# Conditioned layer norms of a graph network: scale and shift as one float32r product over 128 rows

## The chip, the cores and the metric

One core of one Trainium2 chip. The metric is device microseconds of one execution of the whole program; the kernel before takes 2460.31 us (median of 3 runs, 2457.22 to 2461.17).

## The reference, cut to what matters

The program is a chain of four graph networks, each followed by an expert network, on 625 nodes of width 512 (five tiles of 125 nodes). The change concerns the third graph network: four blocks, each with two layer norms whose scale and shift come from a 16-wide condition per node.

```python
emb = jnp.concatenate([jnp.sin(ph), jnp.cos(ph)], axis=-1)
cond = jax.nn.silu(emb @ f_w1 + f_b1) @ f_w2 + f_b2            # (625, 16)
def _cond_layer_norm(x, cond, sw, sb, bw, bb):
    xn = (x - mu) * jax.lax.rsqrt(var + EPS)
    scale = cond @ sw + sb                                     # (625, 512)
    bias = cond @ bw + bb
    return xn * (1.0 + scale) + bias
for i in range(4):
    y = _cond_layer_norm(x, cond, s1_w[i], s1_b[i], b1_w[i], b1_b[i])
    y = _sparse_attention(y, src, dst, wq[i], bq[i], wk[i], bk[i], wv[i], bv[i], wo[i], bo[i])
    x = x + y
    y = _cond_layer_norm(x, cond, s2_w[i], s2_b[i], b2_w[i], b2_b[i])
    x = x + jax.nn.relu(y @ m_w1[i] + m_b1[i]) @ m_w2[i] + m_b2[i]
```

All of it is float32. 4 blocks, 2 norms and 5 tiles make 40 conditioned tiles, each with two products of a (125 x 17) by a (17 x 512) matrix.

## The kernel before, in words

Each network is a block of five hand-ordered instruction streams (TensorE = PE, VectorE = DVE, ScalarE = ACT, GpSimd = POOL, SyncE = SP, which issues the weight loads), joined by semaphores; a barrier ends a block. The order of each stream is the order of the Python code: nothing reorders it.

**The condition.** `b.GT` holds the condition turned, 16 rows and a row of ones, once on partitions 0 to 16 and again on 32 to 48 (ACT, L1472, late in the second layer of the graph network before). `b.affine[n]` holds, for norm n of a block, the weights and bias row of the scale on partitions 0 to 16 (columns 0 to 511) and those of the shift on 32 to 48 (columns 512 to 1023). SP loads them with two transfers (L1827, L1828, L1838, L1839; for the first block L1105), POOL sets the buffers to zero once (L1139), and ACT adds 1 to the scale's bias row in `plus_one` (L2053; L1511 for the first block).

**A conditioned tile** is one call of `cond(layer, n, t)` on PE (L1878; `next_condition(t)`, L1226, for the first three tiles): two float32 products with 32 rows each, one on row group 0 and one on row group 1 of the array (`tile_position=(32 * a, 0)`), into PSUM banks 6 and 7. DVE reads bank 6 in `norm_second` (L2173) and bank 7 in `norm_third` (L2179), which releases `y_ready`; the next `cond` waits for that, since the two banks are used again.

**The third graph network** (`l2_gnn_block`), per block of 4: values, keys and queries; a loop of i = 0 to 22 over 20 pairs (tile, head), in which PE does at step i `score(i)`, `turned(i - 2)` (five transposes), `attend(i - 3)`, at i = 7, 11, ... `project`, at i = 9, 13, 17, 21 `cond(layer, 1, 0..3)`. Beside it DVE adds the mask and takes the maximum (L2232), ACT does the exponential (L2083), DVE `normalise` (L2206), ACT copies the transposes (`turned_out`, L2090). At i = 9, 13, 17 ACT also takes the square root for the norm (`root`, L2060), which needs another function table, and then the exponential's again. After the loop come the dense layers with `cond(layer, 1, 4)` and `cond(layer + 1, 0, 0..4)` between their products. POOL adds bias rows to the residual in `add_row` (L1853).

**The end of the block before** (`l1_gnn_block`): six experts, each five products on PE (L1223) and five accumulations on DVE (`expert_added`, L1636); before the last expert's products PE does `next_condition(0)`; then `last_added`, `output_normed` and `next_norm` on DVE alternate with `next_turned` and `next_value` on PE for tiles 0 to 2.

Of the kernel before, what the change touches and what calls it, by code (L numbers as in the profile page):

```python
# [16 lines left out]
U32 = mybir.dt.uint32  # L17
ALU = mybir.AluOpType
# [80 lines left out]
class Program:  # L99
    def __init__(self, nc, ctx, args):  # L100
        self.nc, self.ctx, self.args = nc, ctx, args
        self.open = []

    def sb(self, name, shape, dt=F32):
        return self.ctx.enter_context(self.nc.sbuf_tensor(name, shape, dt))

# [868 lines left out]
FIRST_NORM = ("plus_one", "cond_mm", "y_ready", "var", "std", "xt_mm", "v_mm", "v_out", "c_act")  # L975
# [3 lines left out]
def l1_gnn_block(nc, p, b, A, hb):  # L979
# [8 lines left out]
                   "added", "cnt_max", "log_ready", "masked", "ovar", "ostd", "o_ready", "affine_zero", "pad_zero")  # L988
# [31 lines left out]
    emb_hidden = b.HT[0:16, 4, :]  # L1020
    c1, c2 = 6.28125, 0.0019340515136718750
# [23 lines left out]
    with nc.Block(no_gpsimd_drain=True) as block:  # L1045
        @block.sync
        def _(sp):
# [21 lines left out]
            sp.dma_start(b.emb_w[0:16, 16:80], A["L2_gnn_f_w2"]).then_inc(s["vec_in"], 16)  # L1069
# [49 lines left out]
        def _(pool):  # L1119
# [17 lines left out]
            pool.wait_ge(s["m2_mm"], T * NL)  # L1137
            for n in range(2):
                nc.gpsimd.memset(b.affine[n], 0.0).then_inc(s["affine_zero"], 1)  # L1139
# [3 lines left out]
        def _(pe):  # L1143
# [82 lines left out]
            def next_condition(t):  # L1226
                if t == 0:
                    pe.wait_ge(g2["plus_one"], 1)
                if t < 2:
                    pe.wait_ge(s["e_out"], E_OUT[NE - 2 + t, 1])  # L1230
                else:
                    pe.wait_ge(s["added"], T * (NE - 1) + 3)
                for i in range(2):
                    last = nc.tensor.matmul(b.ps[0:R, COND[t][i], :], b.GT[32 * i:32 * i + 32, t * R:(t + 1) * R],
                                            b.affine[0][32 * i:32 * i + 32, i * D:(i + 1) * D], start=True, stop=True,
                                            tile_position=(32 * i, 0))
                last.then_inc(g2["cond_mm"], 1)
# [24 lines left out]
            for layer in range(NL):  # L1262
# [51 lines left out]
                if layer == 1:  # L1314
                    pe.wait_ge(s["h1"], 1)
                    embed(b.emb_w[0:16, 16:80], emb_hidden, 64, "cond_mm")
# [50 lines left out]
        def _(act):  # L1367
# [72 lines left out]
            for layer in range(NL):  # L1440
# [29 lines left out]
                if layer == 1:  # L1470
                    act.wait_ge(s["cond_mm"], 1)
                    nc.scalar.activation(halves(b.GT[0:64, :]), b.slot(1)[0:64, :, 0:HF], ACT.Identity,  # L1472
                                         bias=b.cols[0:64, C["f_b2"]:C["f_b2"] + 1]).then_inc(s["cond"], 1)
# [35 lines left out]
            for n in range(2):  # L1509
                act.wait_ge(p.g2_affine[n], 32)  # L1510
                nc.scalar.activation(b.affine[n][0:32, 0:D], b.affine[n][0:32, 0:D], ACT.Identity,  # L1511
                                     bias=b.ident[0:32, 16:17]).then_inc(g2["plus_one"], 1)
# [12 lines left out]
        def _(dve):  # L1525
# [169 lines left out]
            for layer in range(NL):  # L1695
                for t in range(USED):
# [9 lines left out]
                    if layer == 1 and t % 6 == 5 and t < 60:  # L1706
                        angle_step(t // 6)
                for t in range(1, T, 2):
# [31 lines left out]
            for x in range(NE - 1):  # L1740
# [38 lines left out]
def l2_gnn_block(nc, p, b, A):  # L1779
# [5 lines left out]
                   "bo_added", "mb2_added", "stats")  # L1785
# [7 lines left out]
    OT = [b.W[:, 12288 + 512 * u:12288 + 512 * u + KD * R].rearrange("p (k n) -> p k n", k=KD) for u in range(2)]  # L1793
    GA, GB = (0, 3 * R), (3 * R, N)
# [22 lines left out]
    with nc.Block(no_gpsimd_drain=True) as block:  # L1817
        @block.sync
        def _(sp):
# [3 lines left out]
            clear_retired(sp, retired)  # L1823
            for layer in range(NL - 1):
# [13 lines left out]
                sp.dma_start(b.affine[1][0:17, 0:512], sb[:, 1024:1536]).then_inc(p.g2_affine[1], 16)  # L1838
                sp.dma_start(b.affine[1][32:49, 512:1024], sb[:, 1536:2048]).then_inc(p.g2_affine[1], 16)  # L1839
# [12 lines left out]
        def _(pool):  # L1852
# [9 lines left out]

            for layer in range(NL):
# [188 lines left out]
        def _(act):  # L2052
            def plus_one(layer, n):  # L2053
                act.wait_ge(p.g2_affine[n], 32 * (layer + 1))
                nc.scalar.activation(b.affine[n][0:32, 0:D], b.affine[n][0:32, 0:D], ACT.Identity,
# [1477 lines left out]
```

## Time and profile before

| what | value |
|---|---|
| median of 3 runs | 2460.31 us |
| span of the profiled execution, first to last instruction | 2460.5 us |
| PE busy | 2277.9 us (93%) |
| DVE, ACT, POOL busy | 1105.7, 700.9, 616.0 us |
| mean granted TensorE clock | 0.961 |
| third graph network, 1050 to 1735 us: PE busy | 677.9 of 685 us |
| PE instructions of `cond` (L1884) | 148, 41.6 us |

The span is counted from the program's first instruction; all times of rows below are on that axis. A float32 product appears as two pairs of LDWEIGHTS (PEld) and MATMUL (PE), so a conditioned tile is four MATMUL rows. A MATMUL's recorded duration includes the time until its last column has left the array; how fast PE gets through a row of products is read from the distances of their starts.

### The profile page before, as it was taken

The page shows a single profiled execution, that of the slowest core. Times are in us where ns is not written, and L with a number is a line of the kernel's source. Part 1 is how long each engine was busy: PE and PEld are TensorE (multiplying, and loading weights), DVE is VectorE, ACT ScalarE, POOL GpSimd, SP SyncE. Part 2 cuts the span into 40 slices and gives each one's busy share as a digit, 9 for nine tenths or more (in the row PEclk, how much of TensorE's full clock was granted, in tenths as well). Part 3 has the DMA queues.
Part 4 walks back from the last instruction along what each step waited for, and adds up shares of the span by engine and source line. Part 5 has one row for each costly group of instructions (what it writes and reads, how often), then busy time and mean ns, then how long its engine had stood idle before and what let it go on. Part 6 is the DMA issues. An engine that isn't in the chain of part 4 may idle for free. (4 is left out here: it accounts for less than half of the span.)

```text
span 2460.5 us, 35289 instructions
## 1 busy us (share of the span) xinstructions
PE 2277.9 (93%) x12133; PEld 1471.8 (60%) x12133; DVE 1105.7 (45%) x2643; ACT 700.9 (28%) x1366; POOL 616.0 (25%) x625
## 2 busy tenths in 40 slices
PE   5798969999999999999999999999997896989998
PEld 4475547766766765566566576576653333567775
DVE  8733885545545546735325325335442223530102
ACT  0422333323333323225225135135201111112111
POOL 0463666506515520010100100101123442111110
PEclk9898989999999998999999999999989997979999
DMA  3122027517516533010110110110037646458885
GB/s 91 49 68 78 1 64 222 151 31 225 152 43 212 152 100 113 1 61 38 51 68 1 58 60 1 57 52 1 21 141 246 230 169 208 108 217 320 306 298 181
DMA packets 70260, 285.73 MB, mean 116 GB/s; under 512 B 19274, under 2 KB 19402, under 8 KB 62158
## 3 DMA queue, kind: packets, MB, share of 16 engines
q1 hardware_dynamic: 35771, 189.60, 22.0%
q0 software_dynamic: 32448, 91.31, 12.3%
q10 hardware_dynamic: 1872, 2.56, 0.4%
q8 instruction: 107, 1.75, 0.3%
q14 instruction: 62, 0.51, 0.1%
HBM read 407.54 MB, written 26.23 MB: 176 GB/s over the span
## 5 line engine op out<-in xcount | busy, mean ns | idle before, releaser
L86 PE MATMUL ps<-XT,W 128*128 128x250 f32 (+1 forms) x1200 | 335.4, 435 | 3.5 <-ACT XT L1420 1.6
L86 PEld LDWEIGHTS ps<-XT,W 128*128 128x128 f32 x1200 | 229.0, 193 | 106.4 <-issue 22.3
L1150 PE MATMUL ps<-XN,W 128*128 128x512 f32 x498 | 256.8, 598 | 2.6 <-ACT GT L1472 2.6
L1856 POOL TENSOR_TENSOR H<-H,RB 125x512 f32<-125x512 f32 x40 | 50.5, 1266 | 723.9 <-DVE XN L2179 611.6
L86 PE MATMUL ps<-W,HT 128*128 128x512 f32 (+1 forms) x312 | 141.5, 608 | 0.8 <-ACT HT L3293 0.5
L86 PEld LDWEIGHTS ps<-HT,W 128*128 128x128 f32 x1088 | 126.3, 195 | 8.8 <-issue 7.7
L86 PE MATMUL ps<-HT,W 128*128 128x128 f32 x1088 | 126.6, 278 | 0.8 <-DVE HT L3304 0.8
L2567 POOL DMA_INDIRECT result_rows<-KT,LOGC x61 | 61.9, 1016 | 257.0 <-DVE KT L3324 211.7
L1126 POOL DMA_INDIRECT XT<-node_rows,LOGC x81 | 77.3, 954 | 173.8 <-DMA node_rows<-V 122.2
L1288 PEld LDWEIGHTS ps<-P,QT 128*128 128x128 f32 x672 | 89.2, 194 | 44.5 <-issue 44.5
L1288 PEld LDWEIGHTS ps<-P,KT 128*128 128x128 f32 x672 | 88.1, 192 | 39.7 <-issue 39.7
L3293 ACT ACTIVATE HT<-ps,lcols 128x128 f32<-128x128 f32 x136 | 50.1, 368 | 211.1 <-PE ps L86 211.1
L1288 PEld LDWEIGHTS ps<-P,XT 128*128 128x128 f32 x648 | 85.2, 193 | 41.7 <-issue 41.6
L2720 PE MATMUL ps<-W,HT 128*32 128x320 f32 x824 | 109.0, 445 | 0.0
L2232 DVE CUSTOM_DVE_ANT_0 P<-ps,LOGC 125x626 f32<-125x626 f32 x80 | 64.6, 807 | 96.0 <-PE ps L94 96.0
L86 PE MATMUL ps<-HT,V 125*128 125x125 f32 x800 | 102.7, 275 | 0.0
L86 PEld LDWEIGHTS ps<-W,HT 128*128 128x128 f32 (+1 forms) x312 | 58.8, 193 | 72.7 <-issue 67.8
L94 PE MATMUL ps<-KT,QT 128*125 128x313 f32 x320 | 98.8, 430 | 0.0
L1126 POOL DMA_INDIRECT QT<-node_rows,LOGC x84 | 79.7, 949 | 65.5 <-PE ps L1288 41.6
L86 PEld LDWEIGHTS ps<-HT,V 125*128 125x128 f32 x800 | 95.7, 192 | 0.3
L2083 ACT ACTIVATE P<-P,nmax 125x626 f32<-125x626 f32 x80 | 65.4, 818 | 98.9 <-DVE nmax L2237 98.8
L1126 POOL DMA_INDIRECT KT<-node_rows,LOGC x84 | 79.4, 945 | 56.0 <-PE ps L1288 45.1
(654 smaller groups left out, 4422.7 us busy)
## 6 DMA issues: line engine op xcount, KB each, us to landing
W<-in_L_ffn_Wgud SPq DMA_DIRECT2D x103, 896.0 KB
W<-in_L_ffn_w SPq DMA_DIRECT2D x36, 2048.0 KB, 7.9
W<-in_L_gnn_Wqkv SPq DMA_DIRECT2D x4, 3072.0 KB, 10.0
W<-in_L_gnn_W SPq DMA_DIRECT2D x5, 2048.0 KB, 14.4
H<-in_L_ffn_Wgud SPq DMA_DIRECT2D x11, 896.0 KB
XN<-in_L_ffn_Wgud SPq DMA_DIRECT2D x11, 896.0 KB
V<-in_L_ffn_Wgud SPq DMA_DIRECT2D x11, 896.0 KB
P<-in_L_ffn_Wgud SPq DMA_DIRECT2D x11, 896.0 KB
```

Of the source, the lines that this page charges most:

```text
L86: last = nc.tensor.matmul(out, lhs(k), rhs(k), start=(k == 0), stop=(k == nk - 1))
L94: last = nc.tensor.matmul(slot[0:m, a, 0:HF], lhs(k), rhs(k)[:, a * HF:(a + 1) * HF], start=(k == 0), stop=(k == nk - 1))
L1126: nc.gpsimd.indirect_dma_start(edges[n % GR], None, hb, bass.IndirectOffsetOnAxis(ap=b.slot_src[:, t:t + 1], axis=0)).then_inc(arrived[n % ...
L1150: nc.tensor.matmul(b.ps[:, n % PR, :], b.EAT[:, t * 128:(t + 1) * 128], We[layer], start=True, stop=True)\
L1288: last = nc.tensor.matmul(sums[:, k * 128:][:, bass.ds(off, R)], edges[n % GR][:, k * 128:(k + 1) * 128], hot[n % HR], start=False, stop=F ...
L1856: ins = nc.gpsimd.tensor_tensor(b.H[0:R, t, :], b.H[0:R, t, :], b.RB[0:R, at:at + D], ALU.add)
L2083: nc.scalar.activation(P[j % 5], P[j % 5], ACT.Exp, bias=b.nmax[0:R, j:j + 1], accum_out=b.den[0:R, j:j + 1]).then_inc(s["exp"], 1)
L2232: v.tensor_tensor_reduce(out=halves(P[i % 5]), in0=b.slot(0)[0:R, :, 0:HF], in1=halves(b.LOGC[0:R, t, :]), scale=1.0, scalar=-3e38, op0=AL ...
L2567: self.nc.gpsimd.indirect_dma_start(self.rows, bass.IndirectOffsetOnAxis(ap=self.b.slot_row[:, sl:sl + 1], axis=0), out, None, bounds_chec ...
L2720: last = nc.tensor.matmul(b.ps[QUARTER[j], 1 + u % 2, 0:2 * HE], xT[u % 2][:, k, QUARTER[j]], Wgu[4 * (u % WR) + j][:, k, :], start=(k == ...
L3293: nc.scalar.activation(hT[u][:, m, :], b.ps[:, 1 + m % 4, 0:128], ACT.Relu, bias=r.bias[u][:, m:m + 1]).then_inc(s["hidden_ready"], 1)
```

## The change

The condition and the affine weights are kept in two parts each: a high part, rounded to float32r, and the rest, which float32r holds exactly. The four row groups of 32 partitions hold, for the condition, high, rest, high, rest, and for the weights high, high, rest, rest, so that one product over 128 rows sums all four partial products. Scale and shift are then two products, one behind the other, on the whole array. The 1 of `1 + scale` becomes a row of the weights. `plus_one` goes.

Instead of it, per norm: SP loads 18 rows by 1024 columns into each of four row groups of a staging buffer (four transfers in place of two); DVE rounds all 128 x 1024 into `b.affine[n]` (`affine_high`); POOL subtracts on the lower 64 partitions (`split_affine`), after which `cond` may start. The condition is split once, on DVE, in the third layer of the network before. The last network's product with `b.GT` uses its 8 rows alone.

```diff
+    def rounded(self, name, like, shape, column=0):
+        return self.nc.alloc_sbuf_tensor_at(name, shape, F32R, offset=self.start_of[like] + 4 * column)
...
+            sp.wait_ge(s["staged_zero"], 1)
             for n in range(2):
-                sp.wait_ge(s["affine_zero"], n + 1)
-                for part in range(2):
-                    at = 1024 * n + 512 * part
-                    sp.dma_start(b.affine[n][32 * part:32 * part + 17, 512 * part:512 * part + 512],
-                                 A["L2_gnn_sb"][0, :, at:at + 512]).then_inc(p.g2_affine[n], 16)
+                for i in range(4):
+                    sp.dma_start(staged[n][32 * i:32 * i + 18, :], A["L2_gnn_sb"][0, :, 1024 * n:1024 * (n + 1)])\
+                        .then_inc(p.g2_affine[n], 16)
...
+            nc.gpsimd.memset(kt[:, 0:2048], 0.0).then_inc(s["staged_zero"], 1)
             for n in range(2):
-                nc.gpsimd.memset(b.affine[n], 0.0).then_inc(s["affine_zero"], 1)
+                pool.wait_ge(s["affine_high"], n + 1)
+                nc.gpsimd.tensor_tensor(b.affine[n][64:128, :], staged[n][64:128, :], b.affine[n][64:128, :],
+                                        ALU.subtract).then_inc(g2["affine_split"], 1)
...
             def next_condition(t):
                 if t == 0:
-                    pe.wait_ge(g2["plus_one"], 1)
+                    pe.wait_ge(s["cond_split"], 2)
+                    pe.wait_ge(g2["affine_split"], 1)
...
+                    if layer == 2 and t == 5:
+                        v.tensor_copy(b.cond_pair[:, :], cond_rows).then_inc(s["cond_high"], 1)
+                    if layer == 2 and t in (11, 17):
+                        dve.wait_ge(s["cond_high"], 1)
+                        lo = 32 if t == 11 else 96
+                        v.tensor_tensor(b.cond_pair[lo:lo + 32, :], cond_rows[lo:lo + 32],
+                                        b.cond_pair[lo:lo + 32, :], ALU.subtract)\
+                            .then_inc(s["cond_split"], 1)
...
+                if x == 4:
+                    for n in range(2):
+                        dve.wait_ge(p.g2_affine[n], 64)
+                        v.tensor_copy(b.affine[n], staged[n]).then_inc(s["affine_high"], 1)
             last_added(0)
...
                 sp.wait_ge(s["cond_mm"], norm(layer, 0, T - 1))
-                sp.dma_start(b.affine[0][0:17, 0:512], sb[:, 0:512]).then_inc(p.g2_affine[0], 16)
-                sp.dma_start(b.affine[0][32:49, 512:1024], sb[:, 512:1024]).then_inc(p.g2_affine[0], 16)
+                sp.wait_ge(s["affine_split"], 2 * layer + 2)
+                for i in range(4):
+                    sp.dma_start(staged[32 * i:32 * i + 18, :], sb[:, 0:1024]).then_inc(p.g2_affine[0], 16)
...
+            def split_affine(layer, n):
+                pool.wait_ge(s["affine_high"], 2 * layer + n - 1)
+                pool.wait_ge(s["bo_added"], T * layer + 3 if n else T * layer)
+                nc.gpsimd.tensor_tensor(b.affine[n][64:128, :], staged[64:128, :], b.affine[n][64:128, :],
+                                        ALU.subtract).then_inc(s["affine_split"], 1)
...
                     for t in range(T):
                         add_row(layer, n, t)
+                        if t == 2 and n == 0 and layer:
+                            split_affine(layer, 1)
+                    if n == 0 and layer < NL - 1:
+                        split_affine(layer + 1, 0)
...
             def cond(layer, n, t):
                 if t == 0:
-                    pe.wait_ge(s["plus_one"], 2 * layer + n + 1)
+                    pe.wait_ge(s["affine_split"], 2 * layer + n + 1)
...
-                    last = nc.tensor.matmul(b.ps[0:R, 6 + a, :], b.GT[32 * a:32 * a + 32, t * R:(t + 1) * R],
-                                            b.affine[n][32 * a:32 * a + 32, a * D:(a + 1) * D], start=True, stop=True,
-                                            tile_position=(32 * a, 0))
+                    last = nc.tensor.matmul(b.ps[0:R, 6 + a, :], b.cond_pair[:, t * R:(t + 1) * R],
+                                            b.affine[n][:, a * D:(a + 1) * D], start=True, stop=True)
...
+            def affine_high(layer, n):
+                dve.wait_ge(p.g2_affine[n], 64 * (layer + 1))
+                v.tensor_copy(b.affine[n], staged).then_inc(s["affine_high"], 1)
...
                     if i:
                         normalise(layer, i - 1)
+                    if layer and i == 2:
+                        affine_high(layer, 1)
+                    if not final and i == 6:
+                        affine_high(layer + 1, 0)
```

Three places in the order of the streams. **DVE, end of the block before**: L1636 are the experts' accumulations, L1758 an independent mask step; the last of the six L1636 in a row is the first tile of the last expert. Before:

```order
1160 L1758 SCALAR_TENSOR_TENSOR LOGC<-P,LOGC 125x3130
1161 L1636 SCALAR_TENSOR_TENSOR X<-ps,gates,X 125x512 x6
1162 L1648 BN_STATS stats<-X 125x6
1163 L1649 BN_AGGR mv<-stats 125x2
1164 L1636 SCALAR_TENSOR_TENSOR X<-ps,gates,X 125x512
```

Now (L1647 is the line that was L1636):

```order
1163 L1778 SCALAR_TENSOR_TENSOR LOGC<-P,LOGC 125x3130
1164 L1647 SCALAR_TENSOR_TENSOR X<-ps,gates,X 125x512 x5
1165 L1783 CAST affine_pair<-KT 128x1024 x2
1166 L1647 SCALAR_TENSOR_TENSOR X<-ps,gates,X 125x512
1167 L1659 BN_STATS stats<-X 125x6
```

The two roundings stand behind all five accumulations of the fifth expert and ahead of the first of the sixth. **PE at the same place**, L1238 (was L1223) the experts' products, L1250 `next_condition`, L1257 transposes, L87 (was L86) values; the order of the rows is that of before:

```order
3262 L1238 MATMUL ps<-W,HT 125x512 x5
3263 L1250 MATMUL ps<-affine_pair,cond_pair 125x512 x2
3264 L1238 MATMUL ps<-W,HT 125x512 x5
3265 L1250 MATMUL ps<-affine_pair,cond_pair 125x512 x2
3266 L1257 MATMUL ps<-ident,XN 128x125 x4
3267 L1250 MATMUL ps<-affine_pair,cond_pair 125x512 x2
3268 L87 MATMUL ps<-W,XT 125x512 x4
```

What moved is what row 3263 waits for: the subtraction on POOL instead of an addition on ACT. **POOL** from the end of that block into the first two blocks of the third network; L1884 is `add_row`, L1152 and L1894 are the subtractions:

```order
119 L1148 MEMSET KT 128x2048
120 L1152 TENSOR_TENSOR affine_pair<-KT,affine_pair 64x1024 x2
121 L1155 MEMSET KT 128x4
122 L1056 UNCONDITIONAL_BRANCH
123 L1879 UNCONDITIONAL_BRANCH
124 L1898 MEMSET W 128x1024
125 L1884 TENSOR_TENSOR H<-H,RB 125x512 x5
126 L1894 TENSOR_TENSOR affine_pair<-W,affine_pair 64x1024
127 L1884 TENSOR_TENSOR H<-H,RB 125x512 x8
128 L1894 TENSOR_TENSOR affine_pair<-W,affine_pair 64x1024
```

Before, POOL had two memsets of 128 x 1024 in place of the first two rows and nothing between the additions of L1856.

## Rows read from the trace of the kernel before

**Rows 1.** Windows: length, busy us of PE, PEld, DVE, ACT, POOL, clock, DMA.

```profile
1015.00:1050.00 35.00, 32.21 (x85) 14.48 (x84) 27.21 (x46) 6.46 (x14) 0.00 (x0) 0.90 0.00 0
1050.00:1225.00 175.00, 171.77 (x769) 110.58 (x767) 75.21 (x184) 63.02 (x129) 17.59 (x14) 1.00 0.12 43
```

**Rows 2.** Waits of PE, 1040 to 1730: us in total, times, longest.

```profile
PE ps L1939 <- ACT HT L2090: 4.2, 12, 0.3
```

**Rows 3.** Timeline of PE in the first block: start us, us, line, xcount.

```profile
1178.31 5.21 PE L86 MATMUL ps<-XT,W 128*128 128x375 f32 x16
1183.36 1.02 PE L86 MATMUL ps<-W 128*125 128x512 f32 x2
...
1187.93 5.31 PE L86 MATMUL ps<-XT,W 128*128 128x375 f32 x16
1193.17 1.12 PE L1884 MATMUL ps<-W,GT 32*125 32x512 f32 x4
1194.23 1.98 PE L1973 MATMUL ps<-W,HT 128*125 128x512 f32 x4
```

**Rows 4.** 512 columns: line L307 (ns min/median/max, first to last start); timeline, float32.

```profile
L307 PE MATMUL ps<-H x8: 374/374/425, 59.6 to 61.2; 1*125 1x512 bf16 x8
...
1023.56 4.45 PE L1223 MATMUL ps<-W,HT 128*125 128x512 f32 x10
```

**Rows 5.** Timeline, all engines, around step 9 of the loop, first block.

```profile
1126.34 0.82 ACT L2083 ACTIVATE P<-P,nmax 125x626 f32<-125x626 f32 x1 [1.28 <-DVE nmax L2237]
1126.86 1.12 PE L1884 MATMUL ps<-W,GT 32*125 32x512 f32 x4
1127.27 1.28 ACT L2060 ACT_TABLE_LOAD   x1
1128.76 0.67 ACT L2090 ACTIVATE HT<-ps 125x625 f32<-125x625 f32 x1
1129.58 0.78 PE L1939 MATMUL ps<-ident,P 125*125 125x125 f32 x5 [0.34 <-ACT HT L2090]
```

**Rows 6.** Timeline of the end of the block before.

```profile
1024.62 4.18 DVE L1636 SCALAR_TENSOR_TENSOR X<-ps,gates,X 125x512 f32<-125x512 f32 x5 [0.99 <-PE ps L1223]
1027.94 1.12 PE L1234 MATMUL ps<-W,GT 32*125 32x512 f32 x4
1029.00 4.56 PE L1223 MATMUL ps<-W,HT 128*125 128x512 f32 x10
1036.71 1.09 PE L1242 MATMUL ps<-ident,XN 125*128 125x125 f32 x4 [2.11 <-DVE XN L1661]
1037.74 2.07 PE L1234 MATMUL ps<-W,GT 32*125 32x512 f32 x4
1039.74 5.52 PE L86 MATMUL ps<-W,XT 128*125 128x512 f32 x8
```

**Rows 7.** Groups by line and shape: busy us, mean ns.

```profile
L555 DVE COPY P<-CNT 125x626 f32<-125x626 f32 x5 | 2.4, 479 | 0.0
L2179 DVE SCALAR_TENSOR_TENSOR XN<-XN,rstd,ps 125x512 f32<-125x512 f32 x37 | 27.7, 748 | 1.3
L1856 POOL TENSOR_TENSOR H<-H,RB 125x512 f32<-125x512 f32 x40 | 50.5, 1266 | 723.9 <-DVE XN L2179 611.6 <-POOLq L1045 112.3
```

**Rows 8.** Timeline, POOL and DVE in the last block; all of L2206 (ns min/median/max).

```profile
1665.30 1.27 POOL L1860 TENSOR_TENSOR H<-H,X 125x512 f32<-125x512 f32 x1
...
1665.65 1.25 DVE L2206 TENSOR_SCALAR P<-P,den,row_has 125x626 f32<-125x626 f32 x1
...
L2206 DVE TENSOR_SCALAR P<-P,den,row_has x80: 604/606/1255, 1099.8 to 1700.4; 125x626 f32<-125x626 f32 x80
```

**Rows 9.** Timeline of DVE: step 7, step 3 (block 2), edge loop.

```profile
1116.11 0.81 DVE L2232 CUSTOM_DVE_ANT_0 P<-ps,LOGC 125x626 f32<-125x626 f32 x1 [1.23 <-PE ps L94]
...
1283.35 0.60 DVE L2206 TENSOR_SCALAR P<-P,den,row_has 125x626 f32<-125x626 f32 x1
...
787.32 0.69 DVE L1704 TENSOR_TENSOR KT<-KT,ps 128x512 f32<-128x512 f32 x1 [0.87 <-PE ps L1150]
```

More of the change, by code:

```diff
@@ L17 @@
 U32 = mybir.dt.uint32
+F32R = mybir.dt.float32r
 ALU = mybir.AluOpType
@@ L972, in l0_ffn_block @@
     close_retired(retired)
-FIRST_NORM = ("plus_one", "cond_mm", "y_ready", "var", "std", "xt_mm", "v_mm", "v_out", "c_act")
+FIRST_NORM = ("affine_split", "cond_mm", "y_ready", "var", "std", "xt_mm", "v_mm", "v_out", "c_act")
 FIRST_TILES = 3
@@ L1020, in l1_gnn_block @@
     emb_hidden = b.HT[0:16, 4, :]
+    kt = b.KT[:, :, :].rearrange("p k n -> p (k n)")
+    staged = [kt[:, 1024 * n:1024 * (n + 1)] for n in range(2)]
+    cond_rows = b.HT[:, 5, :]
     c1, c2 = 6.28125, 0.0019340515136718750
@@ L1233, in next_condition @@
                 for i in range(2):
-                    last = nc.tensor.matmul(b.ps[0:R, COND[t][i], :], b.GT[32 * i:32 * i + 32, t * R:(t + 1) * R],
-                                            b.affine[0][32 * i:32 * i + 32, i * D:(i + 1) * D], start=True, stop=True,
-                                            tile_position=(32 * i, 0))
+                    last = nc.tensor.matmul(b.ps[0:R, COND[t][i], :], b.cond_pair[:, t * R:(t + 1) * R],
+                                            b.affine[0][:, i * D:(i + 1) * D], start=True, stop=True)
                 last.then_inc(g2["cond_mm"], 1)
@@ L1471, in _ @@
                     act.wait_ge(s["cond_mm"], 1)
-                    nc.scalar.activation(halves(b.GT[0:64, :]), b.slot(1)[0:64, :, 0:HF], ACT.Identity,
-                                         bias=b.cols[0:64, C["f_b2"]:C["f_b2"] + 1]).then_inc(s["cond"], 1)
+                    nc.scalar.activation(halves(cond_rows), b.slot(1)[:, :, 0:HF], ACT.Identity,
+                                         bias=b.cols[:, C["f_b2"]:C["f_b2"] + 1]).then_inc(s["cond"], 1)
             turned_out(2)
@@ L1508, in _ @@
                     nc.scalar.activation(b.LOGC[0:R, :, :], b.P[0:R, :, :], ACT.Ln).then_inc(s["log_ready"], 1)
[L1509 to L1512, printed above, removed]
             row_root("ovar", "ostd", b.std, b.mv, 0)
@@ L1707, in _ @@
                         angle_step(t // 6)
+                    if layer == 2 and t == 5:
+                        dve.wait_ge(s["cond"], 1)
+                        v.tensor_copy(b.cond_pair[:, :], cond_rows).then_inc(s["cond_high"], 1)
[5 more added lines that the diff above has]
+                            .then_inc(s["cond_split"], 1)
                 for t in range(1, T, 2):
@@ L1823, in _ @@
             clear_retired(sp, retired)
+            sp.wait_ge(s["staged_zero"], 1)
             for layer in range(NL - 1):
@@ L1861, in add_row @@
                 ins.then_inc(done, 1)
+            def split_affine(layer, n):
[3 more added lines that the diff above has]
+                                        ALU.subtract).then_inc(s["affine_split"], 1)
+                pool.wait_ge(s["affine_split"], 2 * layer + n + 1)
+            nc.gpsimd.memset(staged, 0.0).then_inc(s["staged_zero"], 1)
             for layer in range(NL):
@@ L2052, in _ @@
         def _(act):
-            def plus_one(layer, n):
-                act.wait_ge(p.g2_affine[n], 32 * (layer + 1))
-                nc.scalar.activation(b.affine[n][0:32, 0:D], b.affine[n][0:32, 0:D], ACT.Identity,
-                                     bias=b.ident[0:32, 16:17]).then_inc(s["plus_one"], 1)
             def root(layer, n, t):
@@ L2107, in _ @@
                         root(0, 0, 4)
-                if layer:
-                    plus_one(layer, 1)
                 for t in range(2):
@@ L2131, in _ @@
                     hidden_out(layer, m, M1A + m, GA, 0)
-                if not final:
-                    plus_one(layer + 1, 0)
                 root(layer, 1, 4)
@@ L3046, in _ @@
             for t in range(T):
-                nc.tensor.matmul(b.ps[0:R, B2_BANKS[t], :], b.GT[:, t * R:(t + 1) * R], B2, start=True, stop=True)\
+                nc.tensor.matmul(b.ps[0:R, B2_BANKS[t], :], b.GT[0:NE, t * R:(t + 1) * R], B2[0:NE, :], start=True,
+                                 stop=True)\
                     .then_inc(s["b2_mm"], 1)
@@ L3409, in build @@
         b.PT = ht[:, 0:T * NP].rearrange("p (t n) -> p t n", t=T)
-        b.affine = [b.W[:, 14336 + 1024 * n:14336 + 1024 * (n + 1)] for n in range(2)]
+        affine_pair = p.rounded("affine_pair", "W", [128, 2048], 14336)
+        b.affine = [affine_pair[:, 1024 * n:1024 * (n + 1)] for n in range(2)]
+        b.cond_pair = p.rounded("cond_pair", "GT", [128, NP])
         at = [0]
@@ L3457, in pad, with padded, affine @@
         return out
-    def twice(x, next_row):
-        out = np.zeros(64, f)
-        for at in (0, 32):
-            out[at:at + 16], out[at + 16] = x, next_row
-        return out
+    def padded(x, ones):
+        out = np.zeros(32, f)
+        out[:16], out[16:18] = x, ones
+        return out
+    def affine(i):
+        parts = []
+        for n, one in (("s1", 1), ("b1", 0), ("s2", 1), ("b2", 0)):
+            parts.append(np.concatenate([a[f"L2_gnn_{n}_w"][i], a[f"L2_gnn_{n}_b"][i][None], np.full((1, D), one, f)]))
+        return np.concatenate(parts, axis=1)
     freq = pad(np.tile(np.arange(1, 33, dtype=f) * f(TWO_PI / 16), 2))
@@ L3467, in _layout @@
             col(a["L0_gnn_be2"]), a["L0_ffn_b1"].T, freq, pad(a["L2_gnn_f_b1"]),
-            pad(twice(a["L2_gnn_f_b2"], f(1)))]
+            np.tile(padded(a["L2_gnn_f_b2"], f(1)), 4)[:, None]]
     out = {
@@ L3487, in _layout @@
         "L1_ffn_w2": np.concatenate(list(a["L1_ffn_w2"]), axis=1),
-        "L2_gnn_f_w1": a["L2_gnn_f_w1"], "L2_gnn_f_w2": np.stack([twice(x, f(0)) for x in a["L2_gnn_f_w2"]]),
-        "L2_gnn_sb": np.concatenate([np.concatenate([a[f"L2_gnn_{n}_w"], a[f"L2_gnn_{n}_b"][:, None, :]], axis=1)
-                                     for n in ("s1", "b1", "s2", "b2")], axis=2),
+        "L2_gnn_f_w1": a["L2_gnn_f_w1"], "L2_gnn_f_w2": np.stack([np.tile(padded(x, f(0)), 4) for x in a["L2_gnn_f_w2"]]),
+        "L2_gnn_sb": np.stack([affine(i) for i in range(4)]),
         "L2_gnn_Wqkv": np.stack([np.concatenate([rows(a[f"L2_gnn_w{n}"][i]) for n in "qkv"], axis=1)
```

20 lines of the change are left out of this document (13 added, 7 removed).

## Prediction, made before the run

> **What bounds the kernel now.** I read the page's busy shares first, then windows over the third graph network. The first of its four blocks shows PE busy 171.8 of 175 us at a granted clock of 1.00, the 2.4 GHz level, with DVE at 75 and ACT at 63 us [rows 1]. The list of who waits for whom confirms it: over the whole network PE loses 4.2 us in 12 waits of 0.3 us, all at the transposes L1939 on ACT's copies, and next to nothing else [rows 2]. So here a microsecond of PE time is a microsecond of the kernel, unless the PE time lies in front of one of those 12 waits. The last 35 us of the block before are different: clock 0.90 and DVE busy 27.2 us, a chain that passes between DVE and PE [rows 1].
>
> **What a conditioned tile costs.** Its four MATMUL rows start at 1193.17 and the next work at 1194.23: 1.06 us [rows 3]. Around it there is more. Sixteen float32 rows of 375 columns between ordinary neighbours go from 1178.31 to 1183.36, 5.05 us; sixteen such rows between two conditioned tiles take 1187.93 to 1193.17, 5.24 us. The 0.19 us are a pause ahead of the 32-row products and one behind them. **A tile costs 1.25 us.** Ten float32 rows of 512 columns take 4.45 us, 0.43 to 0.44 each [rows 4], so four in a row would be 1.7: the two products do run at the same time on their two row groups.
>
> **What it costs afterwards.** No float32r product is in this trace. The nearest below is bfloat16 with 512 columns: eight start between 59.6 and 61.2 us, 0.23 us each, in one row per product [rows 4]. The nearest above is float32, two rows of 0.43 or 0.86 us per product. Two products on the whole array, one behind the other, cost 0.46 us by the first and 1.72 by the second. I take 0.46, since splitting both factors in parts that the type holds exactly only makes sense if the array multiplies what it is given in one pass, and a product over all 128 rows has ordinary neighbours, so the pauses go. Were they to stay, 0.65. Gain per tile: 1.25 - 0.46 = 0.79 us, at least 0.60 if the pauses stay.
>
> The Trainium skill, TensorEngine Tiling (Array Packing), "Key Properties", says that a change of tiling mode drains the engine; the pauses of 0.19 us agree with it, and by it they go.
>
> **How many tiles pay.** 40 tiles, in three groups.
> - 12 pay nothing: those at i = 9, 13 and 17 in four blocks. At i = 9 ACT begins an exponential at 1126.34, before PE begins the tile (1126.86); ACT then loads a table (1127.27), takes the root, copies the transposes (1128.76), and only then may PE transpose again, at 1129.58 after 0.34 us of waiting [rows 5]. Nothing of that ACT chain waits for the tile. A shorter tile makes the wait 0.34 + 0.79 = 1.1 us and the transposes come at the same time. These are the 12 waits of [rows 2].
> - 25 pay in full: two at the start of the first block, four at i = 21, four `cond(layer, 1, 4)`, and fifteen of the next block's first norm. PE meets no wait behind them, and where it meets DVE's result (second tile of a norm) that result is counted from a product that moves forward with it. 25 x 0.79 = **-19.8 us**.
> - 3 lie at the end of the block before, and there something is added.
>
> **The end of the block before.** DVE ends the fifth expert at 1024.62 + 4.18 = 1028.80, while PE began the first conditioned tile already at 1027.94 [rows 6]: its weights had long been ready. Now they are ready only after DVE rounds (behind 1028.80) and POOL subtracts. Rounding 1024 columns: the copy L555 takes 0.48 us for 626 columns [rows 7], so 0.78; the upper bound is L2179's rate, 0.75 us per 512, so 1.5. Subtracting 1024 columns on POOL: twice 1.27 [rows 7], 2.5 us. The first tile starts at 1028.80 + 0.78 + 2.53 and 0.1 to hand over (0.15 between ACT's end and PE in [rows 5]), 1032.2, or at 1033.0 if POOL gets at the data only behind the second rounding; with 0.46 us for the tile the sixth expert's products start at 1032.7 to 1033.4 in place of 1029.00: 3.7 to 4.4 us late. All that follows hangs on them through DVE. Behind it one tile takes 2.07 us, twice the usual, and the next products 5.52 us for eight rows: the low clock level after PE's wait of 2.11 us [rows 6]. That tile shrinks by 1.1 to 1.5 us. The new PE wait of 4 us may call up the low level too, earlier; then the products behind are hit instead, which is worth 2 us either way. Net 0 to 5, I take **+2.5 us**.
>
> The Trainium skill, SBUF — State Buffer, "Who interferes with whom", says that VectorE and GpSimd share one port pair that an instruction holds as a whole. The trace agrees: L2206, 0.606 us in the median, took 1.25 us when POOL's L1860 had begun 0.35 us ahead of it [rows 8]. By this rule the later of the two starts, 1033.0, holds.
>
> **The rest, by what covers it.** Six roundings in the attention loops, at i = 2 and i = 6: DVE has waited 1.23 us for PE before the next step [rows 9], more than 0.78; at 1.5 us a step is 0.3 late, 1.8 us in all at most. Six subtractions on POOL, which is idle for 724 us around its 40 additions [rows 7]; the additions behind them are not wanted before the loop's end. SP gives out four transfers for two and now waits for the subtraction; behind that wait stand the next block's weights, wanted a block (175 us) later. ACT loses eight `plus_one`, for which PE does not wait today: nothing gained. Three DVE instructions in the edge loop of the block before, 0.5 to 0.9 us each by the rows of [rows 7], against a DVE wait of 0.87 us per edge [rows 9]: at most 0.3 us. The five last products with 8 rows have as many columns as before: nothing, or a pause or two. Together **+0.3 us** (0 to 2.5).
>
> **Sum.** 2460.5 - 19.8 + 2.5 + 0.3 = **2443.5 us**, 0.7% faster. The profiled span of 2460.5 us stands at the median of the runs (2460.31), so nothing is to be converted. 0.2% are 4.9 us, about what a measurement of this kernel tells from no change.
>
> **Rivals.**
> - *The float32r product costs what float32 costs.* Then the overlap of the two row groups is given up for nothing: 1.72 us per tile, 0.47 more on 25 tiles (11.8 us); on 12 the wait of 0.34 swallows all but 0.13 (1.6 us); the end of the block before gives 3.8. 2460.5 + 17.2 = **2477.7**, slower. It decides above 0.57 us per product, where 25 x (1.25 - 2p) equals the 2.8 us added. For it: no such row here; against it: the single pass that the split suggests. 0.08. The Trainium skill, TensorE: Matmul & The Clock Gate, "Part 3", counts matmuls on different row groups as simultaneous; the 1.06 us against 1.7 above agree, and it is what the change gives up.
> - *The change does half of what it says*: two rows, 0.43 us per product. 0.86 per tile, gain 0.39 x 25 = 9.8: **2453.5**. 0.08.
> - *POOL holds up the softmax.* The subtraction after i = 2 lasts till about 1284.0 by the same working, and L2206 starts at 1283.35 [rows 9]: it would be held 0.6 us, and PE wants the result a step later, about a microsecond on. If all six subtractions came through in full, 15 us: **2458**, no change. 0.05.
> - *The 12 tiles pay too*, because the ACT chain moves forward in some way that I do not see: 37 x 0.79 = 29.2: **2434**. 0.05.
>
> **Chances.** My forecast 0.74, its own range 2440 to 2451 (0.60 to 0.79 per tile, 0 to 5 and 0 to 2.5 us). Range to hold 8 in 10: 2438 to 2456, which takes in the half case and leaves out 0.18. Faster: 0.74 and 0.05 and half of the half case, 0.83. Same: the rest of that and POOL, 0.08. Slower: 0.09.
>
> **What would show it.** Right: 74 and 6 MATMUL rows for `cond` and `next_condition` in place of 148 and 12, with starts 0.21 to 0.23 us apart; sixteen rows of 375 columns between two tiles in 5.05 us; 12 waits on L2090's successor of about 1.1 us, 13 us in all; PE waiting some 4 us before the first tile at the end of the block before. Wrong: starts 0.43 or 0.86 us apart, the 12 waits still 0.3 us, or new waits of PE for the softmax at i = 4 or i = 8.

## The result, and the profile after

The changed kernel takes 2439.64 us (median of 4 runs, 2437.80 to 2444.14), the kernel before on the same chip 2459.65 us: a ratio of 0.9918, 95% interval 0.9906 to 0.9930, so 17 to 23 us or 0.7 to 0.9% faster. The forecast was 2443.5 us. The profiled execution is the fastest of the four: 2437.8 us, span 2436.1 us, against a span of 2460.5 before. That is a difference of 24.4 us, more than the medians show; where the surplus lies is settled below.

Lines have moved: `cond` is L1924 (was L1884), `next_condition` L1250 (L1234), the transposes of the softmax L1978 (L1939), ACT's copies of them L2124 (L2090), the division of the softmax L2236 (L2206).

**Conditioned tiles.** The groups by line of the changed kernel: engine, operation, count, then min/median/max duration in ns.

```profile
L1924 PE MATMUL ps<-affine_pair,cond_pair x74: 387/439/797, 1055.1 to 1700.1; 128*125 128x512 f32 x74
...
L1250 PE MATMUL ps<-affine_pair,cond_pair x6: 395/434/824, 1030.4 to 1040.2; 128*125 128x512 f32 x6
```

74 and 6 rows in place of 148 and 12: one row per product, so float32r is one pass. The recorded durations (387 to 824 ns) say nothing about their price; the distances do. PE in the first block, at the place of [rows 3]: start us, us, line, xcount.

```profile
1183.34 1.02 PE L1924 MATMUL ps<-affine_pair,cond_pair 128*125 128x512 f32 x2
1184.20 5.20 PE L87 MATMUL ps<-XT,W 128*128 128x375 f32 x16
1188.95 0.92 PE L1924 MATMUL ps<-affine_pair,cond_pair 128*125 128x512 f32 x2
1189.70 0.59 PE L2012 MATMUL ps<-W,HT 128*125 128x512 f32 x1
```

From the sixteen rows of 375 columns to the first product behind the tile it is 1189.70 - 1184.20 = 5.50 us. The same stretch in [rows 3] is 1194.23 - 1187.93 = 6.30. Less the 5.05 of the sixteen rows, a tile costs **0.45 us where it cost 1.25**. (Here the recorded starts mislead: the product at 1188.95 is stamped 0.03 us behind the last row of 375 columns, which itself needs 0.31.)

**The third network**, from its first conditioned tile to the first of its last five accumulations on DVE (1055.99 to 1728.69 before), in windows; columns as in [rows 1]. Before, then after:

```profile
1055.99:1728.69 672.70, 667.39 (x2969) 432.57 (x2970) 274.23 (x669) 243.00 (x490) 56.87 (x45) 1.00 0.11 41
```

```profile
1055.07:1709.04 653.97, 639.41 (x2895) 435.51 (x2896) 277.69 (x675) 239.17 (x484) 72.29 (x52) 1.00 0.12 44
```

18.7 us shorter at the same granted clock of 1.00, with 74 PE rows fewer. PE's busy time falls by 28.0 us, 9 more than the stretch does: those went into waits. PE's waits, 1040 to 1730 us, against [rows 2]:

```profile
PE ps L1978 <- ACT HT L2124: 13.6, 12, 1.1
...
PE ps L1924 <- PEq L1056: 1.1, 1, 1.1
```

The 12 waits behind the tiles of steps 9, 13 and 17 are 1.1 us now, 13.6 in all, and no wait for the softmax has appeared. The place of [rows 5], with ACT's table load:

```profile
1124.36 0.70 PE L1924 MATMUL ps<-affine_pair,cond_pair 128*125 128x512 f32 x2
1124.90 1.22 PE L95 MATMUL ps<-KT,QT 128*125 128x313 f32 x4
1124.94 1.28 ACT L2094 ACT_TABLE_LOAD   x1
...
1126.44 0.67 ACT L2124 ACTIVATE HT<-ps 125x625 f32<-125x625 f32 x1
1127.26 0.78 PE L1978 MATMUL ps<-ident,P 125*125 125x125 f32 x5 [1.14 <-ACT HT L2124]
```

**The end of the block before**, all engines, against [rows 6]:

```profile
1021.64 4.45 PE L1238 MATMUL ps<-W,HT 128*125 128x512 f32 x10
1022.70 4.18 DVE L1647 SCALAR_TENSOR_TENSOR X<-ps,gates,X 125x512 f32<-125x512 f32 x5 [0.99 <-PE ps L1238]
1026.80 1.28 DVE L1783 CAST affine_pair<-KT 128x1024 fp32r<-128x1024 f32 x2
1027.63 5.08 POOL L1152 TENSOR_TENSOR affine_pair<-KT,affine_pair 64x1024 fp32r<-64x1024 f32 x2 [85.92 <-DVE affine_pair L1783]
1030.38 0.70 PE L1250 MATMUL ps<-affine_pair,cond_pair 128*125 128x512 f32 x2 [4.29 <-issue]
1030.91 6.15 PE L1238 MATMUL ps<-W,HT 128*125 128x512 f32 x10
1039.24 0.65 PE L1257 MATMUL ps<-ident,XN 125*128 125x125 f32 x4 [1.68 <-DVE XN L1672]
1039.90 0.73 PE L1250 MATMUL ps<-affine_pair,cond_pair 128*125 128x512 f32 x2
1040.66 3.67 PE L87 MATMUL ps<-W,XT 128*125 128x512 f32 x8
```

PE stands still for 4.29 us until the first subtraction on POOL is done. The ten products behind the stop then run in part at the low clock (6.15 us in place of 4.56), while the tile and the eight products that had run in part at it before (2.07 and 5.52 us) take 0.73 and 3.67. In windows of ten microseconds the granted clock is 0.83 from 1030 on (part of it at 1.2 GHz, the lower of two levels) and 1.00, 2.4 GHz, from 1040 on:

```profile
1030.00:1040.00 10.00, 7.93 (x19) 3.63 (x19) 7.07 (x15) 0.96 (x4) 2.73 (x3) 0.83 0.00 0
1040.00:1050.00 10.00, 8.86 (x26) 3.99 (x26) 9.54 (x21) 2.39 (x6) 0.00 (x0) 1.00 0.00 0
```

From the fifth expert's first product to the third network's first tile it is 33.43 us here, 32.43 before: +1.0.

**What covers the rest.** The roundings and subtractions at the end of the block before and in the loops, and all divisions of the softmax: ns min/median/max, first to last start.

```profile
L1783 DVE CAST affine_pair<-KT x2: 682/683/684, 1026.8 to 1027.4; 128x1024 fp32r<-128x1024 f32 x2
...
L1152 POOL TENSOR_TENSOR affine_pair<-KT,affine_pair x2: 2352/2502/2651, 1027.6 to 1030.4; 64x1024 fp32r<-64x1024 f32 x2
...
L2241 DVE CAST affine_pair<-W x6: 684/686/686, 1112.5 to 1617.0; 128x1024 fp32r<-128x1024 f32 x6
...
L1894 POOL TENSOR_TENSOR affine_pair<-W,affine_pair x6: 2353/2358/2359, 1113.2 to 1617.7; 64x1024 fp32r<-64x1024 f32 x6
...
L2236 DVE TENSOR_SCALAR P<-P,den,row_has x80: 604/606/1044, 1097.5 to 1682.0; 125x626 f32<-125x626 f32 x80
```

### The profile page after: what moved, and what is told of

It is laid out like the page before. It is cut to its first block and busy times, and to the rows that moved or that the text cites. A ratio compares the mean times of both kernels' runs of the same rounds, so it can differ in the third digit from the quotient of the medians.

```text
span 2436.1 us, 35178 instructions
## 1 busy us (share of the span) xinstructions
PE 2245.6 (92%) x12053; PEld 1473.5 (60%) x12053; DVE 1111.6 (46%) x2654; ACT 695.9 (29%) x1358; POOL 637.6 (26%) x633
## 5 line engine op out<-in xcount | busy, mean ns | idle before, releaser
L87 PE MATMUL ps<-XT,W 128*128 128x250 f32 (+1 forms) x1200 | 333.7, 434 | 3.5 <-ACT XT L1435 1.6
L87 PEld LDWEIGHTS ps<-XT,W 128*128 128x128 f32 x1200 | 229.4, 193 | 100.1 <-issue 15.6
L87 PE MATMUL ps<-W,HT 128*128 128x512 f32 (+1 forms) x312 | 141.3, 607 | 0.8 <-ACT HT L3332 0.5
L1884 POOL TENSOR_TENSOR H<-H,RB 125x512 f32<-125x512 f32 x40 | 50.9, 1278 | 314.4 <-DVE XN L2209 314.1
L87 PEld LDWEIGHTS ps<-HT,W 128*128 128x128 f32 x1088 | 126.5, 195 | 8.8 <-issue 7.7
L87 PE MATMUL ps<-HT,W 128*128 128x128 f32 x1088 | 126.8, 278 | 0.8 <-DVE HT L3343 0.8
L87 PE MATMUL ps<-HT,V 125*128 125x125 f32 x800 | 102.7, 275 | 0.0
L87 PEld LDWEIGHTS ps<-W,HT 128*128 128x128 f32 (+1 forms) x312 | 58.6, 193 | 72.7 <-issue 67.7
L87 PEld LDWEIGHTS ps<-HT,V 125*128 125x128 f32 x800 | 95.7, 192 | 0.3
```

The lines of the kernel that those rows point to most:

```text
L87: last = nc.tensor.matmul(out, lhs(k), rhs(k), start=(k == 0), stop=(k == nk - 1))
L1884: ins = nc.gpsimd.tensor_tensor(b.H[0:R, t, :], b.H[0:R, t, :], b.RB[0:R, at:at + D], ALU.add)
```

## Experiments

**1. The changed kernel once more**: is the surplus of the first pair of profiles part of the change? No edit.

> The changed kernel once more. In the first pair of profiles the changed kernel is 24.4 us shorter. Theory: what the change itself does is 17 to 19 us (in the third network 18.7, at the end of the block before +1.0); the other 6.7 us lie in stretches in which the work is unchanged (1.9 ahead of the last experts, 4.8 behind the third network) and are differences between executions. Then this run's third network again takes 654 us from its first conditioned tile to its end, within 0.5, its span comes out anywhere from 2436 to 2444, and at least one of the other stretches differs from the first profile by a microsecond or more. Rival: the 6.7 us belong to the change (fewer loads, or another alignment of the later work). Then all stretches repeat within 0.5 us and the span is 2436 again.

Measured: 2442.81 us (median, 2436.09 to 2448.43), ratio to the kernel before 0.9921, interval 0.9906 to 0.9936; the profiled execution has a span of 2446.7 us. The third network takes 653.9 us again, within 0.1 of the first. All else moved: the fifth expert begins at 1024.54 (1021.64 in the first), the end of the block before takes 35.87 us (33.43), and from the end of the third network's last accumulation to the end of the program it is 709.1 us (703.7), with not a line of difference. So the surplus is not the change's. In the ten profiles of this study that last stretch, in which their code is the same but for line numbers (and, between the kernel before and all others, five products with 8 rows in place of 128), takes 701.9 to 710.7 us: a single profile can be several microseconds off in the whole, while the third network of the changed kernel repeats within a tenth of one.

At the end of the block before the low clock came the second time on the eight products of the values as well, which the first execution had run at the full clock:

```profile
1033.28 1.19 PE L1250 MATMUL ps<-affine_pair,cond_pair 128*125 128x512 f32 x2 [4.29 <-issue]
1034.27 6.23 PE L1238 MATMUL ps<-W,HT 128*125 128x512 f32 x10
...
1042.88 0.65 PE L1257 MATMUL ps<-ident,XN 125*128 125x125 f32 x4 [1.92 <-DVE XN L1672]
1043.54 0.73 PE L1250 MATMUL ps<-affine_pair,cond_pair 128*125 128x512 f32 x2
1044.30 5.37 PE L87 MATMUL ps<-W,XT 128*125 128x512 f32 x8
```

That is 1.7 us of the 2.4 that lie between the two executions; the granted clock of the same two windows is 0.66 and 0.83 here:

```profile
1030.00:1040.00 10.00, 6.72 (x13) 3.26 (x13) 4.58 (x10) 0.59 (x2) 5.11 (x3) 0.66 0.00 0
1040.00:1050.00 10.00, 8.04 (x22) 3.49 (x20) 9.47 (x21) 1.48 (x4) 0.00 (x0) 0.83 0.00 0
```

**2. float32 over 128 rows**: is it the type, or the full array?

```diff
-F32R = mybir.dt.float32r
+F32R = mybir.dt.float32
```

> The same data path, but the type of the condition and of the weights is float32 in place of float32r: the high part is then the whole value and the rest is zero, the two products still go over 128 rows. Theory (the gain is the number of passes of the type): four rows of 0.43 us per tile, 1.72 in place of 0.46, so 1.26 us more on 25 tiles (31.5), 0.16 more on each of the 12 behind which PE waits 1.1 us (1.9), about 3 at the end of the block before: 2439.6 + 36 = 2476 us, slower than the kernel before by 0.7%, and the 12 waits of PE for ACT's copies gone. Rival (the gain comes from the full array and the pauses that go, the type costs the same): 2440 us, and the waits as they are.

Measured: 2476.27 us, ratio 1.0066, interval 1.0051 to 1.0082; slower, as the first theory had it. PE in the first block:

```profile
1211.12 3.60 PE L2012 MATMUL ps<-W,HT 128*125 128x512 f32 x8
1214.56 1.88 PE L1924 MATMUL ps<-affine_pair,cond_pair 128*125 128x512 f32 x4
1216.27 6.92 PE L87 MATMUL ps<-XT,W 128*128 128x250 f32 x32
```

Two rows per product again, 1216.27 - 1214.56 = 1.71 us per tile, and no wait for L2124 is left in the list of waits. Twelve rows in 5.15 us are 0.43 each: on the full array there is no pause. Going over 128 rows is a loss of 0.46 us per tile by itself; that the type goes through in one pass is the whole gain.

**3. float32r with 32 rows, on two row groups, and on one**: to what did the pauses belong? Both leave out three of the four partial products (`cond` shown, `next_condition` alike).

```diff
-    last = nc.tensor.matmul(b.ps[0:R, 6 + a, :], b.cond_pair[:, t * R:(t + 1) * R],
-                            b.affine[n][:, a * D:(a + 1) * D], start=True, stop=True)
+    last = nc.tensor.matmul(b.ps[0:R, 6 + a, :], b.cond_pair[32 * a:32 * a + 32, t * R:(t + 1) * R],
+                            b.affine[n][32 * a:32 * a + 32, a * D:(a + 1) * D], start=True, stop=True,
+                            tile_position=(32 * a, 0))
```

> The changed kernel with its two float32r products in the form of the kernel before: 32 rows each, on row groups 0 and 1. It leaves out the three partial products with a rest. It tells apart what the pause of 0.19 us around a conditioned tile belonged to. Theory 1 (to the 32-row form): the two products run at once in 0.23 us, the pauses stay, 0.42 per tile against 0.46: 1 us less over 25 tiles, 2438 to 2440 us. Theory 2 (to float32): no pauses, 0.23 per tile, 5.8 us less, 2434 us. Theory 3 (float32r products do not overlap on row groups): 0.46 with or 0.65 with pauses, 2440 to 2444 us.

Measured: 2444.78 us, ratio 0.9942, interval 0.9926 to 0.9957; the third network 2.8 us longer than with 128 rows.

```profile
1185.69 0.49 PE L1925 MATMUL ps<-affine_pair,cond_pair 32*125 32x512 f32 x2
1186.11 5.31 PE L87 MATMUL ps<-XT,W 128*128 128x375 f32 x16
1191.35 0.49 PE L1925 MATMUL ps<-affine_pair,cond_pair 32*125 32x512 f32 x2
```

The sixteen rows take 5.24 us again, the 0.19 of pauses that [rows 3] have, so these go with the 32-row form and not with the type. But the tile itself takes 0.42 where the first theory had 0.23: 0.61 with the pauses, 0.15 more than over 128 rows. Two products at once with a further pause, or one behind the other? With both on row group 0:

> The 32-row form once more (three of four partial products left out), but with both products on row group 0, so that they cannot run at once. In e_rows32 the two began 3 ns apart and the next work 0.42 us after them, about the time of two such products one behind the other (0.46). Theory 1 (on two groups they did run at once, 0.22, and 0.2 of the 0.42 is a pause): now 0.62 to 0.65 from the first start to the next work. Theory 2 (two groups gave float32r nothing): again 0.42.

```profile
1187.03 0.72 PE L1925 MATMUL ps<-affine_pair,cond_pair 32*125 32x512 f32 x2
1187.68 5.31 PE L87 MATMUL ps<-XT,W 128*128 128x375 f32 x16
1192.91 0.73 PE L1925 MATMUL ps<-affine_pair,cond_pair 32*125 32x512 f32 x2
1193.57 6.70 PE L2014 MATMUL ps<-W,HT 128*125 128x512 f32 x15
```

Measured: 0.65 us from the first start to the next work; the whole took 2452.49 us in its only execution. The first theory fits: on two groups they ran at once, with 0.2 us on top. The same 0.2 us stands in all three 32-row forms: 0.42 less one product of 0.22, 0.65 less two of them, and 1.06 in the kernel before [rows 3] less two rows of 0.43 [rows 4], where four rows one behind the other would need 1.7. It does not grow with the number of passes, one or two. With the 0.19 outside, a 32-row tile carries about 0.4 us of pauses in each form; where inside the tile the 0.2 lie, the recorded starts do not settle.

**4. Roundings two experts earlier**: what the end of the block before costs.

```diff
-                if x == 4:
+                if x == 2:
                     for n in range(2):
                         dve.wait_ge(p.g2_affine[n], 64)
```

> The changed kernel with the first two roundings on DVE moved from behind the fifth expert to behind the third, where DVE has waited 2.6 us for PE. Theory (the end of the block before costs what PE waits for rounding and subtraction): the 4.3 us wait of PE ahead of the first conditioned tile goes to 0.2 or less, the last expert's ten products take 4.45 us in place of 6.15, PE's wait at the first transposes grows from 1.7 to about 2.8 us and the low clock comes there; from the first product of the fifth expert to the first conditioned tile of the third network 30.7 to 32.4 us in place of 33.4: 1 to 2.7 us faster than the changed kernel, 2437 to 2439 us. Rival (the chain of DVE, not the wait, sets that end): the wait only moves to the first transposes, 33.4 us as before, 2440 us.

```profile
1024.30 4.45 PE L1238 MATMUL ps<-W,HT 128*125 128x512 f32 x10
1028.19 1.02 PE L1250 MATMUL ps<-affine_pair,cond_pair 128*125 128x512 f32 x2
1029.06 4.45 PE L1238 MATMUL ps<-W,HT 128*125 128x512 f32 x10
...
1036.67 0.65 PE L1257 MATMUL ps<-ident,XN 125*128 125x125 f32 x4 [2.67 <-DVE XN L1672]
1037.34 0.99 PE L1250 MATMUL ps<-affine_pair,cond_pair 128*125 128x512 f32 x2
1038.13 5.10 PE L87 MATMUL ps<-W,XT 128*125 128x512 f32 x8
```

The stop is gone, the ten products take 4.45 us, and the wait at the transposes is 2.7 us with the low clock behind it, as expected (granted 0.88 and 0.95 in the two windows of experiment 1). The stretch takes 29.65 us: 2.8 less than before the change, 3.8 and 6.2 less than in the two executions of the changed kernel, somewhat more than forecast. The other executions bear it out: 29.59 us with the early roundings of experiment 6, 33.27 with the late ones and 32.51 in the kernel before, both of experiment 5. Whole: 2437.81 us, ratio 0.9913, interval 0.9899 to 0.9926; on the same chip the changed kernel gave 2442.81, and the intervals overlap, so here the stretch decides and not the total.

**5. No table load in the loops**, in the changed kernel and in the one before: why 12 tiles paid nothing. The root of the loop's tiles becomes a function that every table holds (12 roots are left out).

```diff
-                nc.scalar.activation(b.std[0:R, t:t + 1], b.mv[0:R, t, 1:2], ACT.Sqrt, bias=b.eps5[0:R, :])\
+                of = ACT.Identity if n and t < 3 else ACT.Sqrt
+                nc.scalar.activation(b.std[0:R, t:t + 1], b.mv[0:R, t, 1:2], of, bias=b.eps5[0:R, :])\
```

> The changed kernel, but for the first three tiles of each block's second norm ACT passes the variance on as it is in place of taking its root, so that no function table is loaded between exponentials; it leaves out 12 roots. Theory (the 12 tiles inside the loops paid nothing because ACT's table load sets when PE may transpose again): 1.28 us less on ACT per step against 1.1 us of waiting, so the 12 waits of PE go, 13.6 us: 2439.6 to 2442.8 less 13.6, 2426 to 2429 us; third network 654 less 13.6, 640.4 us from its first conditioned tile to its end. Rival (something else, the softmax on DVE or the banks, holds the transposes): PE waits on at that place for another releaser, and less than half of the 13.6 us come.

> The kernel before with the same edit, the same 12 roots left out. Theory: only its 12 waits of 0.34 us go, 4.2 us: 2459.9 - 4.2 = 2455.7 us; third network 672.7 less 4.2, 668.5 us. Then, without the table loads, the change as a whole shortens the third network by 28 us (37 tiles at 0.75 to 0.79) in place of 18.7. Rival: the third network gains the same in both kernels, and the difference between them stays at 18 to 20 us.

Measured: 2425.09 us (ratio 0.9860, interval 0.9845 to 0.9875) and 2454.15 us (0.9973, 0.9962 to 0.9984). The third network in windows, the changed kernel, then the kernel before, both with the edit:

```profile
1055.79:1693.14 637.35, 636.60 (x2895) 436.15 (x2896) 278.16 (x675) 207.08 (x460) 73.06 (x52) 1.00 0.13 45
```

```profile
1055.88:1721.37 665.49, 664.58 (x2969) 433.51 (x2970) 272.97 (x669) 210.94 (x466) 57.74 (x45) 1.00 0.11 41
```

665.49 - 637.35 = **28.1 us**, as the theory has it, where with the table loads it is 18.7; the waits of PE for ACT's copies are gone in both. (The 654 us that the expectations name is this stretch.) Each kernel gained 3 us more than its waits add up to: 7.2 and 16.6 over 12 places, 0.60 us each where 0.34 of waiting were recorded, 1.39 where 1.13 were. The difference of the two, 0.79 us, is just what a tile became cheaper.

**6. A version that beats both**: experiment 4, and the 12 roots on POOL, which is idle there, in small steps; nothing is left out. `step` issues one operation on POOL behind the one before it.

```diff
+            def root(layer, t):
+                var, y, a = (b.newton[0:R, u:u + 1] for u in range(3))
+                pool.wait_ge(s["var"], norm(layer, 1, t))
+                step(var, b.mv[0:R, t, 1:2], 1e-5, None, ALU.add, ALU.bypass)
+                step(y.bitcast(I32), var.bitcast(I32), -0.5, 1597463007.0, ALU.mult, ALU.add)
+                for u, three in enumerate((3.0, 12.0, 768.0)):
+                    step(a, y, y, var, ALU.mult, ALU.mult)
+                    if u < 2:
+                        step(y, a, three, y, ALU.subtract, ALU.mult)
+                pool.wait_ge(s["steps"], steps[0])
+                nc.gpsimd.tensor_scalar(b.std[0:R, t:t + 1], a, three, y, ALU.subtract, ALU.mult).then_inc(s["std"], 1)
...
+                    c.link(v.tensor_scalar(b.rstd[0:R, t:t + 1], b.std[0:R, t:t + 1], -1.0 / 8192, None, ALU.mult))
-                    if i in (9, 13, 17):
-                        root(layer, 1, i // 4 - 2)
```

> A version that should beat both, with the reference's results: the roundings behind the third expert as in e_early, and the 12 roots of the loops taken on the otherwise idle POOL, in eight small steps (a first guess from the bits and three Newton steps) in place of ACT's table function; DVE's reciprocal there becomes a multiplication. Theory: e_early less the 13.6 us of waits, 2437.8 - 13.6 = 2424 us, range 2422 to 2429. Rival: the eight dependent steps on POOL take longer than the 3 us between the variance and the second half of the norm on DVE; then DVE waits, the next mask and the next scores are late, and part or all of the gain is gone, 2430 to 2440 us.

Measured: **2422.26 us, ratio 0.9846, interval 0.9833 to 0.9860**: 39 us faster than the kernel before on the same chip, 17 to 21 faster than the medians of the change, which were taken on other chips. POOL and DVE at step 9 of the first block:

```profile
1121.79 0.26 POOL L1897 TENSOR_SCALAR newton<-mv 125x1 f32<-125x1 f32 x1 [9.40 <-DVE mv L2220]
1122.12 2.69 POOL L1897 TENSOR_SCALAR newton<-newton 125x1 int32<-125x1 int32 x6
1124.91 0.29 POOL L1909 TENSOR_SCALAR std<-newton 125x1 f32<-125x1 f32 x1
...
1125.24 0.15 DVE L2229 TENSOR_SCALAR rstd<-std 125x1 f32<-125x1 f32 x1 [0.56 <-POOL std L1909]
```

The rival is half there: eight steps take 3.4 us and DVE waits 0.56 for them, but PE does not feel it; the third network takes 637.3 us (1051.87 to 1689.16), as with the roots left out.

## Why the prediction was right

- **A tile costs 1.25 us, then 0.46**: right (1.25 and 0.45), and with it the choice of the bfloat16 row as the nearest price for float32r [rows 4]. The reading of the 0.19 us as "a pause ahead of the 32-row products and one behind them" was too narrow: by experiment 3 another 0.2 us lies inside the 1.06, so the pauses make about 0.4 us per tile. The Trainium skill, TensorEngine Tiling (Array Packing), "Key Properties", puts the drain down to a change of tiling mode; the trace agrees in that the 0.4 us are the same for one 32-row pass and for two, though no run shows that the change of mode is their cause. The sum does not depend on it. The argument that a split in exactly held parts makes sense only with a single pass came out right on the pass (one row per product); that float32r holds the rest exactly, no run shows.
- **25 tiles pay, 12 don't**: right. 18.7 us came in place of 19.8. By the shift between the two traces, most paying tiles gave 0.78 to 0.80, the four at i = 21 gave 0.73 to 0.74, the very first, behind PE's wait of 1.1 us at the start of the network, 0.62, and the second tile of the next block's first norm 0.73, 0.51 and 0.54 in the three blocks. At those last the step "that result is counted from a product that moves forward with it" failed: the chain on DVE between is as long as before, PE comes to its end earlier and loses about 0.26 us there in two of the three blocks (the list of waits shows none). For the 12 the cause is shown, not only argued: without ACT's table load the change is worth 28.1 us in this network, which is what 37 tiles at about 0.76 make.
- **The end of the block before, +2.5 us, 0 to 5**: inside the bounds, +1.0 and +3.4 in two executions. Its pieces were near: rounding 0.68 (0.78 forecast), subtraction 2.35 (2.53), PE's stop 4.29 (4), the sixth expert's products 3.8 us later than before, counted from the fifth's (3.7 to 4.4). What parts the two executions is the clock: behind the stop the low level falls on products of the sixth expert that had run at the full one, and the eight products behind may or may not be spared it (3.67 and 5.37 us; the tile ahead of them took 0.73 both times). An estimate from the starts of these rows, with the full-clock ones of experiment 4 beside them: the low level cost this stretch 3.1 us in the kernel before, and 0.7 and 3.2 in the two executions. Without it the change costs 3.4 us both times, and the early roundings of experiment 4 save 1.1 of their 2.8; that the first profile showed only +1.0 was luck.
- **POOL starts only behind the second rounding**: the step failed. POOL's first subtraction begins at 1027.63, inside the second rounding (1027.40 to 1028.08), and takes 2.65 us in place of 2.35. The price of sharing was 0.3 us, where 0.45 us of the second rounding were left and the forecast had a whole one (0.78).
- **The rest, +0.3 us**: nothing of it is to be seen. Three of the 80 softmax divisions take 1.04 us, each begun while a subtraction on POOL was under way, and PE waits for none of them. The Trainium skill, SBUF — State Buffer, "Who interferes with whom", says that the engine that issues second is blocked; the trace agrees in kind: the division at 1114.88 begins while the subtraction of 1113.23 to 1115.58 runs, and takes 0.44 us more than usual, though 0.70 of that subtraction lay ahead by its recorded end.
- **Sum**: 18.7 less 1.0 or 3.4 make 15.3 to 17.7 us; the forecast was 17.0. The medians of two series lie 20.0 and 17.1 us under the kernel before; from the first pair of profiles alone (24.4) one would have drawn a wrong balance. The first median, 2439.64, lies just under the forecast's own range of 2440 to 2451, whose terms add up to 2440.7 to 2453.0, and inside the wider 2438 to 2456; that the forecast's middle came within 1 us of the second median, 2442.81, is in part luck: its terms missed by 1.1 us, by 1.5 or 0.9, and by 0.3, and some of that cancelled. Of the chances, "same" adds up to 0.09 and "slower" to 0.08, the other way round than stated.
- The rivals: float32's price would have given 2477.7 us, and experiment 2, which makes just that, gave 2476.3.

## What to carry to other kernels

Price a product by the distance to the next work over a stretch that both traces have, never by its recorded duration or start. Before counting a saving in front of a wait, look for what ends that wait: it was ACT's table load that kept 12 of 37 tiles from paying, and taking it away was worth 16.6 us, nearly as much as the change. And preparation that moves to other engines belongs where they wait anyway: two experts earlier it cost nothing, and put last it stopped PE for 4.3 us, with the low clock behind the stop.

## What was not expected of the hardware

- A PE wait costs more than its recorded idle time: 0.60 us for 0.34 and 1.39 for 1.13, in 24 waits 0.26 us more each. The idle time is counted from the modelled end of the last product, which would explain it; no run tests that. The two second tiles above that gave 0.51 and 0.54 lost about the same.
- With 32 rows, float32r on two row groups gains less than it loses: 0.61 us for two products at once with the pauses, 0.46 for the two one behind the other over 128 rows.
- Eight dependent operations on 125 single values take 3.4 us on POOL, 0.4 us each.
